# A four-layer graph network: panel copies bunched, look-ups behind the panels, layer-norms in two halves, sums gathered at once

## What is computed

```python
h = jnp.maximum(_layernorm(x), 0.0); x = x + _L0(h, edge_index, W, a, gamma, beta)   # attention over edges, layer-norm
h = jnp.maximum(_layernorm(x), 0.0); x = x + _L1(h, edge_attr_8, edge_attr_64, ...)  # per-edge MLPs, softmax, segment sum
h = jnp.maximum(_layernorm(x), 0.0); x = x + _L2(h, W, a_src, a_dst, b, src, dst)    # attention
h = jnp.maximum(_layernorm(x), 0.0); x = x + _L3(h, attn_w, src, dst)                # attention, elu
```

## Time and profile before

| | |
|---|---|
| Median of 3 runs | 4504.2 us (4502.95 to 4504.42) |
| The profiled execution | 4507.54 us |
| its span, first to last instruction | 4505.7 us |
| Granted TensorE clock, mean | 0.893 |
| Busy: PE, DVE, ACT, POOL | 74%, 85%, 47%, 41% |
| HBM traffic | 149 GB/s over the span |

### The profile page before, as it was taken

How to read it: one execution, slowest core, us unless ns; L and a number is a source line. 1 busy time by engine, 2 the same in 40 slices (tenths; PEclk the granted TensorE clock), 3 DMA queues, 4 the chain that set the end, 5 groups by cost and what they waited for, 6 DMA issues and landing times. The chain is left out here.

```text
span 4505.7 us, 66927 instructions
## 1 busy us (share of the span) xinstructions
PE 3315.2 (74%) x20105; PEld 1477.1 (33%) x20105; DVE 3811.3 (85%) x6835; ACT 2138.5 (47%) x4380; POOL 1855.8 (41%) x3682
## 2 busy tenths in 40 slices
PE   5555553246569999999991699999999997157166
PEld 2111111111134444444440244444444443122122
DVE  8999987499868888888888788888888886799898
ACT  6999884067423343333340244444444442066076
POOL 0000334400076776777770366666666665000000
PEclk9999887577779999999995799999999998589589
DMA  4654899866345555555550233333333332445545
GB/s 174 256 208 159 280 287 288 247 227 205 116 112 145 140 142 148 138 144 147 144 139 14 61 92 91 92 92 93 93 93 93 92 91 66 160 179 197 197 165 178
DMA packets 404532, 674.29 MB, mean 150 GB/s; under 512 B 71581, under 2 KB 317917, under 8 KB 392529
## 3 DMA queue, kind: packets, MB, share of 16 engines
q1 hardware_dynamic: 338384, 566.65, 38.8%
q0 software_dynamic: 39680, 78.78, 7.0%
q10 hardware_dynamic: 26112, 24.58, 1.8%
HBM read 398.98 MB, written 270.79 MB: 149 GB/s over the span
## 5 line engine op out<-in xcount | busy, mean ns | idle before, releaser
L713 POOL DMA_INDIRECT arena<-h_table,gidx x808 | 783.9, 970 | 311.4 <-issue 236.0
L810 PE MATMUL banks<-arena 128*128 128x500 bf16 x1440 | 392.8, 400 | 308.6 <-DVE arena L1428 177.0
L1717 DVE TENSOR_TENSOR arena<-banks,arena 128x512 f32<-128x512 f32 x808 | 536.7, 685 | 62.4 <-PE banks L903 42.7
L1837 DVE TENSOR_TENSOR arena<-banks,arena 128x512 f32<-128x512 f32 x808 | 518.6, 683 | 36.8 <-PE banks L1013 13.1
L1845 DVE TENSOR_TENSOR arena<-banks,arena 128x512 f32<-128x512 f32 x808 | 516.6, 681 | 0.3 <-PE banks L1019 0.3
L1142 ACT ACTIVATE arena<-arena,h 128x128 bf16<-128x128 f16 x1440 | 454.6, 386 | 90.1 <-DVE arena L1453 47.6
L1293 ACT ACTIVATE arena<-banks 64x256 f32<-64x256 f32 x808 | 305.1, 378 | 339.9 <-PE banks L1045 332.8
L1033 PE MATMUL banks<-arena 128*64 128x256 f32 x3232 | 437.9, 392 | 0.5 <-DVE arena L1847 0.5
L667 POOL DMA_INDIRECT arena<-slots,slot_i x157 | 169.9, 1082 | 651.3 <-DMA slots<-arena 612.5
L1019 PE MATMUL banks<-arena 64*128 64x512 f32 x1616 | 435.2, 616 | 1.5 <-DVE arena L1845 1.2
L909 PE MATMUL banks<-arena 128*64 128x256 f32 x3232 | 429.2, 387 | 0.0
(11 more groups left out here) (289 smaller groups left out, 6400.7 us busy)
## 6 DMA issues: line engine op xcount, KB each, us to landing
arena<-c_flat SPq DMA_DIRECT2D x75, 1562.5 KB, 6.8
slots<-arena SPq DMA_DIRECT2D x90, 1000.0 KB, 4.4
arena<-hs_dump SPq DMA_DIRECT2D x404, 128.0 KB
arena<-mask_rows SPq DMA_DIRECT2D x50, 781.2 KB, 4.3
arena<-in_edge_attr SPq DMA_DIRECT2D x202, 128.0 KB
arena<-placed SPq DMA_DIRECT2D x202, 128.0 KB
xs_dump<-arena SPq DMA_DIRECT2D x202, 128.0 KB
hs_dump<-arena SPq DMA_DIRECT2D x202, 128.0 KB
```

The lines of the kernel that those rows point to most:

```text
L713: pool.indirect_dma_start(out=xs[par][:, k * D:(k + 1) * D], out_offset=None, in_=h_table, in_offset=bass.IndirectOffsetOnAxis(ap=gidx[par ...
L810: last = pe.matmul(ps[4 + r % 2][:, 0:BW], row_hot[r][:, k * P:(k + 1) * P], col_hot[r][:, k * BW:(k + 1) * BW], start=k == 0, stop=k == K ...
L1717: V.tensor_tensor(bt[j], ps[5 + j % 2][:, :], h2k[t % 2], ALU.mult).then_inc(bt_sb, 1)
L1837: V.tensor_tensor(dt_[j % 2], ps[3 + j % 2][:, :], xat[t % 3], ALU.mult).then_inc(dt_sb, 1)
```

## The change

- `copied_after` puts a panel's four quarters after steps 237+16g, +2, +4 and +6, `stored_after` their stores at steps 240+16g, +4, +8, +12 of ACT's program. Stores that would fall behind the last step (two of panel 7) go to SP's queue.
- POOL gathers panels up to 11, then does seven look-ups, gathers panel 12, and does the other 18; there are seven buffers for them. DVE does copies 10, 11 and 12 and the layer-norm before all 25 counts.
- `norm` works on blocks 0 to 13 and 14 to 24 one after the other, and with it what stands around it between layers; who waits for h (PE, POOL) waits for each half. SP's store of h waits for both.
- The carries are no longer added to `run_rows`: they are scattered to a table by node, `carry_rows`, which was zeroed at the start, behind nine gathers of sums; SP reads the table back and DVE adds it. Their indices take three operations behind the counts; five others go from the setup.
- The barrier between layers 2 and 3 goes.

The diff, cut to its core:

```diff
+HALVES = ((0, 14), (14, NB))
...
+    carry_rows = nc.dram_tensor("carry_rows", (HROWS, D), F32).ap()
...
         found = [m_row[:, i * W:(i + 1) * W].bitcast(I32) for i in range(3)]
+        found += [arena[:, NP + i * W:NP + (i + 1) * W].bitcast(I32) for i in range(4)]
+        NF = len(found)
...
         def copied_after(g, i):
-            return 4 * (58 + 4 * g + i) + 1
+            return 4 * (59 + 4 * g) + 1 + 2 * i
+        def stored_after(g, i):
+            return 4 * (60 + 4 * g + i)
...
 # SP
+            sp.dma_start(carry_rows.rearrange("(p b) f -> p (b f)", p=P), zeros[:, 0:HROWS // P * D]).then_inc(carry_zeroed, 16)
...
-            for g in range(INSIDE, PANELS):
+            for g in range(PANELS):
                 for i in range(4):
-                    store_panel(g, i)
+                    if stored_after(g, i) >= SL:
+                        store_panel(g, i)
...
-            sp.wait_ge(h_ready, 2)
+            sp.wait_ge(h_ready, 4)
             sp.dma_start(h_table[0:NP, :].rearrange("(b p) f -> p b f", p=P), h[:, :, :]).then_inc(table_out, 16)
...
             barrier(sp, 4)
+            sp.wait_ge(carry_out, 16)
+            sp.dma_start(agg[:, :, 0:D], carry_rows[0:NP, :].rearrange("(b p) f -> p b f", p=P)).then_inc(carries_in, 16)
             barrier(sp, 5)
             for k, layer in enumerate((2, 3)):
+                if k:
+                    sp.wait_ge(pv_done, PV * 2)
                 load_pass(mask_rows, mask4, mask_in, maxed, NB * k)
                 load_pass(c_rows, ctile, c_in, p_ready, NB * (1 + k))
-                barrier(sp, 6 + k)
+            barrier(sp, 6)
...
 # POOL
             def find_rows(lo, hi):
                 for b in range(lo, hi):
-                    if b >= 3:
-                        pool.wait_ge(row_counted, b - 2)
+                    if b >= NF:
+                        pool.wait_ge(row_counted, b - NF + 1)
...
-            for g in range(INSIDE + 3):
+            for g in range(INSIDE + 4):
                 gather_panel(g)
...
+            landed(SL // 4 - 1)
             pool.wait_ge(rows_ready, 1)
-            find_rows(0, 3)
-            gather_panel(INSIDE + 3)
-            find_rows(3, 9)
+            find_rows(0, NF)
             gather_panel(INSIDE + 4)
-            find_rows(9, NB)
+            find_rows(NF, NB)
...
-            pool.wait_ge(h_ready, 2)
             for b in range(NB):
+                if b in (0, HALVES[1][0]):
+                    pool.wait_ge(h_ready, 3 if b == 0 else 4)
                 pool.indirect_dma_start(out=placed, out_offset=bass.IndirectOffsetOnAxis(ap=start_i[:, b:b + 1], axis=0),
                                         in_=h[:, b, :], in_offset=None).then_inc(placed_out, 16)
...
             barrier(pool, 4)
-            pool.wait_ge(chain_d, 14)
-            pool.indirect_dma_start(out=run_rows, out_offset=bass.IndirectOffsetOnAxis(ap=first_end[:, 0:1], axis=0),
-                                    in_=carryc[:, :], in_offset=None, compute_op=ALU.add, oob_is_err=True).then_inc(carry_out, 16)
-            pool.wait_ge(carry_out, 16)
-
             for b in range(NB):
+                if b == 9:
+                    pool.wait_ge(chain_d, 14)
+                    pool.indirect_dma_start(out=carry_rows, out_offset=bass.IndirectOffsetOnAxis(ap=carry_i[:, 0:1], axis=0),
+                                            in_=carryc[:, :], in_offset=None).then_inc(carry_out, 16)
                 pool.indirect_dma_start(out=got[:, b, :], out_offset=None, in_=run_rows,
-                                        in_offset=bass.IndirectOffsetOnAxis(ap=end_i[:, b:b + 1], axis=0)).then_inc(sums_in, 16)
+                                        in_offset=bass.IndirectOffsetOnAxis(ap=end_i[:, b:b + 1], axis=0)).then_inc(sums_in[b >= HALVES[1][0]], 16)
...
 # PE
             def node_stage(k, layer):
-                pe.wait_ge(h_ready, layer + 1)
                 for b in range(NB):
-                    last = pe.transpose(ps[b // 4][0:D, (b % 4) * P:(b % 4 + 1) * P], h[:, b, :], ident)
+                    if b in (0, HALVES[1][0]):
+                        pe.wait_ge(h_ready, 2 * layer + (1 if b == 0 else 2))
+                    last = pe.transpose(ps[(4 + b // 4) % 8][0:D, (b % 4) * P:(b % 4 + 1) * P], h[:, b, :], ident)
...
 # ACT
-            stores = {min(copied_after(g, i) + 4, SL - 1): (g, i) for g in range(INSIDE) for i in range(4)}
+            stores = {stored_after(g, i): (g, i) for g in range(INSIDE) for i in range(4)}
...
-            deviation(2)
-            deviation(3)
+            for part in range(2):
+                deviation(3 + 2 * part, part)
+                deviation(4 + 2 * part, part)
...
 # DVE
-            do(V.scalar_tensor_tensor(junk_w, dsti[:, :], firstc[:, 0:1], ones[:, 0:1].to_broadcast([P, W]), ALU.is_equal, ALU.mult, accum_out=firstc[:, 1:2]))
...
+            def norm(src, dest, n, part, relu=0):
+                r = slice(*HALVES[part])
+                do(V.tensor_reduce(out=stat[:, 0, r], in_=src[:, r, :], op=ALU.add, axis=AX))
+                do(V.tensor_scalar(stat[:, 1, r], stat[:, 0, r], 1.0 / D, None, ALU.mult))
...
-            count_rows(0, 6)
             for i in range(4):
                 copy_panel(INSIDE + 2, i)
-            count_rows(6, 9)
-            node_stage(0, 0)
+            for part in range(2):
+                norm(x, h, 1 + part, part, 1 + part)
             for i in range(4):
                 copy_panel(INSIDE + 3, i)
-            count_rows(9, 15)
+            projections(0)
             for i in range(4):
                 copy_panel(INSIDE + 4, i)
-            count_rows(15, NB)
+            for b in range(NB):
+                dve.wait_ge(row_found[b % NF], 16 * (b // NF + 1))
...
+            do(V.tensor_scalar(firstc[:, 1:2], nid[:, 0:1], float(NP), firstc[:, 0:1], ALU.add, ALU.subtract))
+            do(V.scalar_tensor_tensor(firstc[:, 1:2], firstc[:, 1:2], nfull[:, 1:2], firstc[:, 0:1], ALU.mult, ALU.add))
+            do(V.tensor_copy(out=carry_i[:, :], in_=firstc[:, 1:2]))
...
+            for part in range(2):
+                r = slice(*HALVES[part])
+                row = [P, r.stop - r.start, D]
+                collect(0, D, part)
+                do(V.tensor_tensor(h[:, r, :], agg[:, r, 0:D], feat[:, r, :], ALU.add))
+                norm(h, h, 3 + 2 * part, part)
...
+                norm(x, h, 4 + 2 * part, part, 3 + part)
...
-            dve.wait_ge(sums_in, NB * 16)
-            do(V.tensor_tensor(got, got, bc(exist[:, :]), ALU.mult))
-            do(V.tensor_tensor(x[:, :, :], x[:, :, :], got, ALU.add))
-            barrier(dve, 5)
+            for part in range(2):
+                r = slice(*HALVES[part])
+                dve.wait_ge(sums_in[part], (r.stop - r.start) * 16)
+                dve.wait_ge(carries_in, 16)
+                do(V.tensor_tensor(got[:, r, :], got[:, r, :], bc(exist[:, r]), ALU.mult))
+                do(V.tensor_tensor(got[:, r, :], got[:, r, :], agg[:, r, 0:D], ALU.add))
+                do(V.tensor_tensor(x[:, r, :], x[:, r, :], got[:, r, :], ALU.add))
+                if part:
+                    barrier(dve, 5)
+                norm(x, h, 7 + part, part, 5 + part)
```

More of the change, by code:

```diff
@@ L321, in build @@
         first_in = [sem(f"first_in{i}") for i in range(2)]
-        row_found = [sem(f"row_found{i}") for i in range(3)]
+        row_found = [sem(f"row_found{i}") for i in range(NF)]
         row_counted = sem("row_counted")
@@ L366, in build @@
         run_out = [sem(f"run_out{i}") for i in range(2)]
-        carry_out, sums_in = sem("carry_out"), sem("sums_in")
+        carry_zeroed, carries_in = sem("carry_zeroed"), sem("carries_in")
+        carry_out, sums_in = sem("carry_out"), [sem(f"sums_in{i}") for i in range(2)]
         x_ready, x_out = sem("x_ready"), sem("x_out")
@@ L1110, in _, with deviation @@
                 back(1 + k, D + 1)
-                barrier(pe, 6 + k)
+            barrier(pe, 6)
         @block.scalar
         def _(act):
-            def deviation(n):
+            def deviation(n, part):
+                r = slice(*HALVES[part])
                 act.wait_ge(ln_var, n)
-                act.activation(stat[:, 3, :], stat[:, 2, :], ACT.Sqrt, bias=eps[:, :], scale=1.0 / D).then_inc(ln_std, 1)
+                act.activation(stat[:, 3, r], stat[:, 2, r], ACT.Sqrt, bias=eps[:, :], scale=1.0 / D).then_inc(ln_std, 1)
             def node_stage(k):
@@ L1123, in node_stage @@
                     act.wait_ge(ht_ps, NJ * k + j + 1)
[L1124 removed]
+                    act.activation(ht[:, j * COLS:j * COLS + n], ps[(4 + j) % 8][0:D, 0:n], ACT.Copy).then_inc(ht_sb, 1)
                 for j in range(NJ) if k == 0 else ():
@@ L1178, in _ @@
                     store_panel(*stores[s])
-            deviation(1)
+            for part in range(2):
+                deviation(1 + part, part)
             node_stage(0)
@@ L1347, in _ @@
                 if layer == 3:
-                    act.wait_ge(act_q, 3)
```

(48 more changed lines are left out.)

93 lines of the change are left out of this document (33 added, 60 removed).

## The result

The changed kernel takes 4433.4 us (median of 4 runs, 4429.5 to 4437.8) where the kernel before, beside it, takes 4504.3 (4 runs, 4503.0 to 4509.1): a ratio of 0.984, interval 0.982 to 0.986, or 71 us less. The forecast was 4436. Its profiled execution spans 4436.0 us against 4505.7, 69.7 less.

The account below looks back on a forecast made before the run. The step loop was taken as bound by DVE with DMA right behind, the tail by DMA and POOL's issuing. -20 -25 -10 -13 +0.4 = -68 us off the 4504.2 us median gave 4436 us, range 4414 to 4465.

Parts of the forecast that it names:

- The loop, -20: Step loop: copies and stores of panels within six steps remove DVE's window waits, -20 us, bounds 0 and -31.3.
- two thirds: Step loop: share of the 31.3 us of copy waits expected to go, giving -20 us.
- 98% of the 334 that the saturated stretch gave: Step loop: without the wait, 10.3 MB must go in 31.2 us, 329 GB/s, against 334 GB/s reached at full DMA share.
- a landing of 7.7 us to begin: Step loop, slower case: DVE starts waiting for a flushed buffer once a flush takes 7.7 us to land.
- the 9.3 that it named as deciding: Step loop, slower case: flush landings over 9.3 us would cancel the other parts' 48 us, at 1.6 us per batch.
- the rival: Step loop, slower: each of 31 batches waits for its flush; at 10.3 us landings 81 us lost, 4537 us; chance 0.03.
- that the whole wait would go: Step loop: at about 358 GB/s, 10.3 MB need an estimated 28.7 us, so the copy waits vanish, -31 us.
- Look-ups behind the panels, -25: Tail before layer 0: look-ups behind panels, seven buffers; last count at 871 instead of 895.6, net -25 us, bounds -33 and -12.
- Norm in halves, 0 to 1, -10: Seam between layers 0 and 1: POOL's scatters start after the first half of the norm, -10 us, bounds -11.7 and -7.
- Sums at once, -13: Seam between layers 1 and 2: gathers of sums start as the barrier opens, -13 us, bounds -15 and -8.
- The conflict set at 2 us: Seam between layers 1 and 2: two gathers' worth of port conflict between POOL and DVE, 2 us off the gain.
- 2 to 3, +0.4: Seam between layers 2 and 3: halves cost extra operations but shorten PE's part, net +0.4 us, bounds -1 and +2.

## Why the prediction was right, step by step

**The total.** The forecast was -68 and the medians give -71, but the terms do not add up to that: the four that the prediction put at -20, -25, -10 and -13 measured -15.3, -24.2, -10.5 and -11.9 in the two profiles, -61.9 together, and 11.1 us came in pass 1 of layer 1, which was in no term. That 4433 lies so near 4436 is in part luck.

**The loop, -20.** Measured -15.3 in the first profile and -21.3 for the steps alone. Nine profiles of kernels with these steps and no added traffic end the loop between 714.6 and 728.0, 723.7 on average: -18.4. In the time the steps are worth 29, by both runs that separate them. The size of the loop's end held; the reason did not: I took two thirds because "98% of the 334 that the saturated stretch gave" would be asked of DMA. The run with more bytes moved 334 GB/s for 246 us, and the changed tail 364 for 35 us. Of the 2.7 us that a panel takes beyond the 31.2 of DVE's own work, 2.0 are waits for flushes that land late; they leave beside a store and behind five gathers in a row, and which of the two delays them is not shown. Two steps' shift of the stores took the waits at the totals from 13.9 to 0.5 us and the panel to 32.0. The prediction had seen the stores beside the flushes and the point from which it costs ("a landing of 7.7 us to begin"); the landings were 10.6 at worst, beyond the 9.3 that it named as deciding, but only one batch in four made DVE wait, 7 of 31, and so 14 us were given back and not 81. The price per batch was right (10.6 less 7.7 is 2.9, the longest wait); the rival had the number of such batches wrong.

The Trainium skill ("DMA: Bandwidth & Descriptors", section "Where 436 GB/s comes from") gives about 358 GB/s of HBM traffic per core. By these traces the tail stood above it, at 364 for 35 us and, on the third chip, at 378 for 30 us; the measurement decides. The estimate that the prediction worked out from it, that the whole wait would go, is nearer to the loop with the later stores (-28) than to the changed kernel's in its first profile.

**Look-ups behind the panels, -25.** Measured -24.2 up to layer 0's pass. The order of events was the forecast one: copy 10 at 775.7 (forecast 793 less 20), the norm's halves 784.4 to 797.4 (13.0 us for 13.5), copy 12 from 816.7, the last count at 855.3 (851). That DMA would set that end was wrong: the counts begin at 821.7 and take 25 times 1.17 us with 5.7 of waiting, nearly all of it for the first refill, so DVE sets that end, after the wait for the last windows. The run with the old steps has this part by itself: its tail is 21.7 us shorter than before (153.5 to 131.8), and some 3 us of the 24.2 belong to the new steps. Three buffers would have cost 16.9 of the gain, on the second chip; what the order is worth on the first was not measured.

**Norm in halves, 0 to 1, -10.** Measured -10.5. First scatter 19.5 us behind the collect, forecast 18.1 behind its own start; 12 scatters beside the norm took 17.0 us, 12 behind it 15.1, so running beside DVE cost 1.9 where 1.7 had been set aside. With POOL held until both halves were ready, the seam took 14.5 us longer. Four of these scatters took 1.17 to 1.47 us instead of 0.95 to 1.00. The Trainium skill ("SBUF — State Buffer", section "SBUF: two separate sides") has one of DVE (with two SBUF inputs) and GpSimd lock the shared ports for a whole instruction. The trace agrees for these four issues and shows most of the others untouched; no run here takes the ports apart from other causes.

**Sums at once, -13.** Measured -13.2 from the barrier to the start of the projections (61.1 to 47.9), and -11.9 up to layer 2's scan, because the projections then run 1.4 us longer at the lower clock. The sum had no term for that. Behind the barrier: first gather 0.2 us, carries' scatter 11.5, their read 13.7, first half 20.2 (forecast 20.4), second 36.6 (34.2), projections 47.9. The conflict set at 2 us was 2.2 (two issues of 1.8 us and one of 1.4). Had the carries been taken first, POOL would have waited 5.9 us; that run cost 3.0 to 4.0.

**2 to 3, +0.4.** Measured -1.2 from the collect to the start of the projections (30.5 to 29.3), and +0.6 up to layer 3's scan, since the projections take 1.8 us longer. So the +0.4 is met by two terms that the sum did not have. One is the clock; the other is ACT's table load, 1.3 us: before, it stood behind DVE's variance, now it comes at 4091.5, 11 us before the square root. The removed barrier may be why, which no run separates. The end gained 1.0.

**What was in no term.** Pass 1 of layer 1 is 11.1 us shorter with the same code. The other profiles of the first chip's runs give 1105.7 to 1108.4, one of them with this part of the kernel as before. Before itself was profiled once (1114.7), in an execution whose time is usual for it (4507.5), so the 6 to 11 us may be chance of that one profile or a real effect of what comes earlier; the cause is open. Without it the stages give -59, and the medians 71 on the first chip, 70 and 67 on the others; which stage holds the difference the single profiles don't settle.

## What to carry to other kernels

When a wait is removed by bunching work, look at which transfers then leave together with one that a buffer depends on. Here a 1 MB flush landed in 10.5 us beside a store and behind five gathers in a row, and in 4.4 us with the store beside it and no gathers in the 7 us before. Stores two steps away evened the gathers out, landings were 6.2 to 8.5 us but for the loop's first panel, and DVE's waits for flushes were nearly gone; a shorter time of the whole kernel was not shown. For small indirect reads, count how many must be in flight to cover a landing: three were too few for counts of 1.17 us each (28.3 us of waiting), seven left one landing of 4.7 us that is waited for, which reordering moved and did not remove; nothing between was tried. Where one engine prepares what another issues one by one, give it the first half as soon as it is there: the gain here was the second half's work less a few slower issues. And where PE gets its work in two halves, look at its granted clock behind the gap: the matmuls that follow can be slower than before.

## What was not expected of the hardware

The same kernel took 4433 us on one chip and 4957 and 5007 on two others, nearly all of it in one stage (525 of 533 us between the profiles of the first and second, 566 of 566 for the third). Pass 1 of layer 1 on the first chip and on the second, a stretch of each (columns as above):

```profile
1300.00:2300.00 1000.00, 981.35 (x7888) 473.97 (x7886) 879.79 (x2143) 398.95 (x834) 720.79 (x742) 1.00 0.53 145
```

```profile
1300.00:2800.00 1500.00, 1183.37 (x7964) 539.72 (x7966) 888.23 (x2166) 399.57 (x844) 707.61 (x748) 0.87 0.37 97
```

The same work (7888 and 7964 matmuls) in 1000 and in 1500 us; PE at a granted clock of 1.00 and 0.87 of full, and busy 98% and 79% of it, so the clock is not all. On the third chip the waits of that stage that have a name are these:

```profile
POOL arena L729 <- DVE gidx L1731: 530.0, 112, 7.7
ACT arena L1247 <- remote: 376.6, 57, 10.9
DVE arena L1737 <- remote: 337.1, 95, 8.6
```

"remote" is a release for which the profile shows no engine of this core. The tail shows the like: on the third chip ACT's copies behind PE's transposes stood 10.6 us for nothing that the profile shows and 3.6 for "remote", PE stood 16.2 us before the projections, and the tail took 140.5 us where the first chip took 128.5. It is not a single case: with the new order DVE waits 11.6 to 17.1 us for the projections in every profile of these two chips, and 1.3 to 3.2 on the first. What holds the engines there was not looked into.
